# Queries and keys of each head as two float32r parts, with two heads in the halves of the partitions and GpSimd fetching them

## The reference

```
xn = layernorm(x, gamma, beta)
q, k, v = heads of xn @ Wq.T / 4, xn @ Wk.T, xn @ Wv.T      # 16 heads of 16
scores = q @ k.T + rel[h, clip(i - j, 0, 128)], masked to i >= j
y = softmax(scores) @ v ;  out = x + y @ Wo.T
```

## Time and profile before

| | us |
|---|---|
| median of 3 runs | 2771.97 |
| the profiled execution | 2777.85 |
| its span | 2776.0 |
| TensorE busy | 2217.6 |
| VectorE busy | 1620.4 |
| ScalarE busy | 969.2 |
| GpSimd busy | 453.9 |
| granted TensorE clock, mean | 0.863 |

### The profile page before, as it was taken

How to read it: one execution, slowest core, us unless ns; L and a number is a source line. 1 busy time by engine, 2 the same in 40 slices (tenths; PEclk the granted TensorE clock), 3 DMA queues, 4 the chain that set the end, 5 groups by cost and what they waited for, 6 DMA issues and landing times.

```text
span 2776.0 us, 39998 instructions
## 1 busy us (share of the span) xinstructions
PE 2217.6 (80%) x13342; PEld 1613.4 (58%) x13342; DVE 1620.4 (58%) x4577; ACT 969.2 (35%) x1964; POOL 453.9 (16%) x402
## 2 busy tenths in 40 slices
PE   4489999908999857999994276378999999999476
PEld 2478888806888736888883144324444454444254
DVE  6744443353555675433444897266866766875695
ACT  4122233203333331232331331325555556556321
POOL 4320000040000134000003553411011011000242
PEclk8799999958999878999997555669999999999755
DMA  7110101020000122001002100242322323230001
GB/s 237 41 59 26 28 28 32 22 76 1 1 1 1 35 83 73 28 28 32 28 28 60 49 12 0 61 65 59 48 42 53 48 47 63 37 43 2 5 22 39
DMA packets 83735, 114.14 MB, mean 41 GB/s; under 512 B 12162, under 2 KB 74020, under 8 KB 80420
## 3 DMA queue, kind: packets, MB, share of 16 engines
q1 hardware_dynamic: 77396, 94.53, 15.5%
q0 software_dynamic: 6144, 17.05, 1.9%
HBM read 68.90 MB, written 42.64 MB: 40 GB/s over the span
## 4 chain that ended last, share of the span: by engine, by line
PE 63%; DVE 21%; ACT 5%; issue 5%; DMA 3%; POOL 2%; another core or an unknown queue 1%; SPq 0%; ACTq 0%; DVEq 0%; POOLq 0%
PE psum L774 9%; PE psum L776 9%; PE psum L775 9%; PE psum L122 5%; PE psum L2097 4%; PE psum L123 4%; PE psum L124 4%; PE psum L2076 4%; PE psum L2056 3%; PE psum L861 3%; PE psum L2080 3%; DVE junk L1961 2%; PE psum L1426 2%; DVE m L1949 1%; DVE stats L155 1%
## 5 line engine op out<-in xcount | busy, mean ns | idle before, releaser
L1898 ACT ACTIVATE pt<-psum 128x512 f32<-128x512 f32 (+3 forms) x768 | 338.9, 491 | 283.2 <-DVE psum L1987 196.2
L739 DVE SCALAR_TENSOR_TENSOR h<-psum,xg,sg 128x128 f32<-128x128 f32 x592 | 166.9, 345 | 415.2 <-PE psum L861 415.2
L774 PE MATMUL psum<-w_hi,xt_hi 128*128 (+1 forms) x720 | 286.3, 398 | 33.7 <-DVE xt_lo L704 33.7
L548 ACT ACTIVATE sg<-psum 128x512 f32<-128x512 f32 x180 | 107.6, 598 | 584.0 <-PE psum L776 543.0
L775 PE MATMUL psum<-w_lo,xt_hi 128*128 (+1 forms) x720 | 284.5, 395 | 0.0
L776 PE MATMUL psum<-w_hi,xt_lo 128*128 (+1 forms) x720 | 284.5, 395 | 0.0
L2056 PE MATMUL psum<-ks,qs 96*128 96x512 bf16 (+3 forms) x768 | 232.9, 342 | 49.7 <-DMA ks<-qk_scr 19.9
L2076 PE MATMUL psum<-qs,ks 99*128 99x512 bf16 (+3 forms) x768 | 236.8, 332 | 18.4 <-ACT pt L1898 11.4
L774 PE MATMUL psum<-w_hi,ht_hi 128*128 (+1 forms) x720 | 220.5, 306 | 8.3 <-DVE x L754 8.0
L1961 DVE CUSTOM_DVE_ANT_0 junk<-psum,band_q 128x256 bf16<-128x256 f32 (+1 forms) x512 | 204.8, 400 | 22.3 <-PE psum L2056 12.0
L776 PE MATMUL psum<-w_hi,ht_lo 128*128 (+1 forms) x720 | 205.9, 286 | 0.0
(11 more groups left out here) (281 smaller groups left out, 4884.4 us busy)
## 6 DMA issues: line engine op xcount, KB each, us to landing
xg<-w_dram SPq DMA_DIRECT2D x54, 256.0 KB, 3.3
qk_scr<-parts SPq DMA_DIRECT2D x32, 384.0 KB, 2.5
qs<-qk_scr SPq DMA_DIRECT2D x96, 128.0 KB, 7.0
ks<-qk_scr SPq DMA_DIRECT2D x96, 128.0 KB, 7.7
xg<-rows_in SPq DMA_DIRECT2D x74, 132.0 KB, 2.2
rows_out<-yb SPq DMA_DIRECT2D x74, 128.0 KB, 1.7
x<-x_dram SPq DMA_DIRECT2D x4, 1024.0 KB, 9.3
out_dram<-x SPq DMA_DIRECT2D x4, 1024.0 KB, 4.4
```

The source lines that it names most:

```text
L739: ins = dve.scalar_tensor_tensor(out=h[i % 2][:, e, :], in0=u[:, e, :], scalar=xg[j % XSLOT][:, at:at + 1], in1=sg[i % 2][:, e, :], op0=AL ...
L774: pe.matmul(out, a[0], b[0], start=first, stop=False)
L1898: act.activation(pt[n % NPT][:, 0:q1 - q0], st_bank(n)[:, 0:q1 - q0], ACT.Exp).then_inc(*exped.up())
```

## The change

Queries and keys are kept as two float32r parts instead of three bf16 ones. ScalarE writes the first part and VectorE the second, so the second copy of ScalarE and the subtraction of GpSimd are gone. A head's stack has 3 x 16 = 48 rows (and 2 rows of the maximum in two float32r parts: 50 instead of 99). Heads 0 and 1 of a unit stand in partitions 0 to 63, heads 2 and 3 in 64 to 127. The maxima stream issues the products of head hh and head 2+hh one after the other, and the scores come in pairs (heads 3, 1 and heads 2, 0), with the bias products behind the pair as a token of their own (`band`). The steps of maxima now stand ahead of a pair, not behind a score; the stream leads by 1.4 units and is filled up to that lead at once. A projection token follows each second pair.

The fetches move from SyncE to GpSimd, and so does the transfer of the maxima into `qs`, now two transfers. The store of the parts stays on SyncE (512 KB instead of 384 KB each). The constant rows of `ks` are written by two copies of 32 rows x 2048 for each slot; they and the first three fetches stand ahead of the first `max_zero` in GpSimd's order. The custom instruction of VectorE writes into the PSUM bank that it reads, and its wait for the one before is gone. The diff, with up to 12 blanks of indentation taken off and cut to its core:

```diff
-HEAD_OF = (HG - 1, *range(HG - 1))
+HALF_ROWS = P // 2
+PAIR = HG // 2
+HEAD_OF = (HG - 1, 1, 2, 0)
+QK_PARTS = [(0, 0), (0, 1), (1, 0)]
+ROWS = DH * len(QK_PARTS)
+NPART = 2
...
+    yield [("max_zero", u)]
+    for hh in range(PAIR):
         for i in QORDER:
-            step = [("max_far", (u, h, i))] if spans(i)[3] else []
-            yield first + step + [("max", (u, h, i))]
-            first = []
+            if spans(i)[3]:
+                yield [("max_far", (u, half * PAIR + hh, i)) for half in range(2)]
+            yield [("max", (u, half * PAIR + hh, i)) for half in range(2)]
     yield [("max_row", u)]
...
-    yield [("max_rest", (u, 1))]
-    yield [("max_part", (u, 2))]
     yield [("max_out", u)]
...
-            yield [("score", (u, cell, pos))]
+        for pos in range(0, HG, 2):
+            yield [("score", (u, cell, pos)), ("score", (u, cell, pos + 1)), ("band", (u, cell, pos))]
...
-order = sum(project(0), []) + [("load", u) for u in range(min(NR, NHG))]
+order = [("ones", 0)] + sum(project(0), []) + [("load", 0)]
+for u in range(1, NR):
+    order += [("ones", u), ("load", u)]
...
-more()
-order.append(("ones", 0))
-steps, lead = HG * NCELL, 1.5
-per_u = HG * BT + 7
+steps, lead = PAIR * NCELL, 1.4
...
     for tokens in attend(u):
-        order.extend(tokens)
         if tokens[0][0] == "value":
+            order.extend(tokens)
             placed.add(tokens[0])
             continue
-        if taken[0] < (u + lead + step / steps) * per_u:
+        while taken[0] < min((u + lead + step / steps) * per_u, len(stream)):
             more()
+        order.extend(tokens)
         order.extend(next(tail, []))
-        if step % 3 == 0:
+        if step % 2 == 0:
             order.extend(next(proj, []))
...
-    qk_scr = nc.dram_tensor("qk_scr", (2, 2, 3, D, SEQ), BF16, kind="Internal").ap()
-    m_scr = nc.dram_tensor("m_scr", (2, 3, HG * BT, P), BF16, kind="Internal").ap()
+    qk_scr = nc.dram_tensor("qk_scr", (2, 2, NPART, D, SEQ), F32R, kind="Internal").ap()
+    m_scr = nc.dram_tensor("m_scr", (2, NPART, HG * BT, P), F32R, kind="Internal").ap()
...
-    qs = [sb(st, f"qs{i}", [KS_ROWS + MROWS, HG, SEQ], BF16) for i in range(NR)]
-    ks = [sb(st, f"ks{i}", [KS_ROWS + MROWS, HG, SEQ], BF16) for i in range(NR)]
+    qs, ks = ([sb(st, f"{n}{i}", [P, PAIR, SEQ], F32R) for i in range(NR)] for n in ("qs", "ks"))
+    unit = sb(st, "unit", [P, 1])
...
-    pt = [sb(st, f"pt{i}", [P, BANK]) for i in range(NPT)]
+    widest = [max(min((c + 1) * BANK, SEQ) - max(j * P, c * BANK) for j, c in CELLS[i::3]) for i in range(3)]
+    pt = [sb(st, f"pt{i}", [P, widest[i // HG]]) for i in range(NPT)]
...
-    parts = sb(st, "parts", [P, 3, KD, CH], BF16)
+    parts = sb(st, "parts", [P, NPART, KD, CH], F32R)
...
-    junk = sb(st, "junk", [P, 2 * P], BF16)
...
-    mparts = sb(st, "mparts", [HG * BT, 3, P], BF16)
+    mparts = sb(st, "mparts", [HG * BT, NPART, P], F32R)
...
+    def half_of(h):
+
+        return h // PAIR * HALF_ROWS, h % PAIR
...
-                sp.wait_ge(*part2(i + 1))
+                sp.wait_ge(*qk_lo(i + 1))
                 sp.dma_start(qk_scr[b % 2, n, :, o * P:(o + 1) * P, c * CH:(c + 1) * CH].rearrange(
-                    "i p s -> p i s"), parts[:, :, o, :]).then_inc(*S.dma(f"scr_out{n}{o}").up())
-            elif kind == "load":
-                b, g = divmod(i, NHG)
-                par, slot = b % 2, i % NR
-                for n in range(2):
-                    for o in range(KD):
-                        sp.wait_ge(*S.dma(f"scr_out{n}{o}")(CB * (b + 1)))
-                if i >= NR:
-                    sp.wait_ge(*score((i - NR + 1) * NCELL * HG))
-                for s0, pair in enumerate(SLOTS):
-                    for n, dst in enumerate((qs[slot], ks[slot])):
-                        src = qk_scr[par, n, pair[n], g * HG * DH:(g + 1) * HG * DH, :]
-                        sp.dma_start(dst[s0 * DH:(s0 + 1) * DH, :, :].rearrange("p h s -> p (h s)"),
-                                     src.rearrange("(d h) s -> d (h s)", h=HG)
-                                     ).then_inc(*S.dma(f"stack_in{slot}").up())
+                    "i p s -> p i s").bitcast(F32), parts[:, :, o, :].bitcast(F32)).then_inc(*S.dma(f"scr_out{n}{o}").up())
...
+                sp.wait_ge(*max_part(NPART * (i + 1)))
+                sp.dma_start(m_scr[i % 2].rearrange("i c p -> c i p").bitcast(F32),
+                             mparts[:, :, :].bitcast(F32)).then_inc(*S.dma("m_out").up())
...
-            elif kind == "qk":
-                bc, n, o, _ = qk_of(i)
-                pool.wait_ge(*part1(i + 1))
-                pool.tensor_tensor(parts[:, 2, o, :], rests[o][:, :], parts[:, 1, o, :],
-                                   ALU.subtract).then_inc(*part2.up())
+            elif kind == "load":
+                b, g = divmod(i, NHG)
+                slot = i % NR
+                pool.wait_ge(*ones_ok(2 * slot + 2))
+                for n in range(2):
+                    for o in range(KD):
+                        pool.wait_ge(*S.dma(f"scr_out{n}{o}")(CB * (b + 1)))
+                if i >= NR:
+                    pool.wait_ge(*score((i - NR + 1) * NCELL * HG))
+                for s0, pair in enumerate(QK_PARTS):
+                    for n, dst in enumerate((qs[slot], ks[slot])):
+                        for half in range(2):
+                            r0 = half * HALF_ROWS + s0 * DH
+                            src = qk_scr[b % 2, n, pair[n], (2 * g + half) * PAIR * DH:
+                                         (2 * g + half + 1) * PAIR * DH, :]
+                            pool.dma_start(dst[r0:r0 + DH, :, :].rearrange("p h s -> p (h s)"),
+                                           src.rearrange("(d h) s -> d (h s)", h=PAIR)
+                                           ).then_inc(*S.dma(f"stack_in{slot}").up())
+            elif kind == "max_out":
+                pool.wait_ge(*S.dma("m_out")(i + 1))
+                for half in range(2):
+                    r0 = half * HALF_ROWS + ROWS
+                    src = m_scr[i % 2][:, half * PAIR * BT:(half + 1) * PAIR * BT, :]
+                    pool.dma_start(qs[i % NR][r0:r0 + NPART, :, :].rearrange("i h s -> i (h s)"),
+                                   src.rearrange("i c p -> i (c p)")
+                                   ).then_inc(*S.dma(f"m_in{i % 2}").up())
...
             elif kind == "ones":
-                pool.wait_ge(*max_zero(1))
-                for r, k in enumerate(ks):
-                    pool.memset(k[KS_ROWS:KS_ROWS + MROWS, :, :], 1.0).then_inc(*ones_ok.up())
-                    pool.wait_ge(*ones_ok(r + 1))
+                if i == 0:
+                    pool.memset(unit[:, :], 1.0).then_inc(*S("unit").up())
+                    pool.wait_ge(*S("unit")(1))
+                else:
+                    pool.wait_ge(*xt_lo(KD * CB))
+                for half in range(2):
+                    rows = slice(half * HALF_ROWS + MQ, half * HALF_ROWS + 2 * MQ)
+                    pool.tensor_copy(ks[i][rows, :, :], unit[rows, :].unsqueeze(2).to_broadcast(
+                        [MQ, PAIR, SEQ])).then_inc(*ones_ok.up())
+                    pool.wait_ge(*ones_ok(2 * i + half + 1))
...
                 act.wait_ge(*proj(bc * PROJ + i % (2 * KD) + 1))
                 act.activation(parts[:, 0, o, :], mx_ring.bank((kind, i)), ACT.Copy,
-                               scale=scale).then_inc(*part0.up())
-                act.wait_ge(*rest_ok(i + 1))
-                act.activation(parts[:, 1, o, :], rests[o][:, :], ACT.Copy).then_inc(*part1.up())
+                               scale=scale).then_inc(*qk_hi.up())
...
-                if n == 0:
-                    dve.wait_ge(*xt_lo(KD * bc + o + 1))
-                else:
-                    dve.wait_ge(*part2(i - KD + 1))
-                dve.wait_ge(*part0(i + 1))
-                dve.scalar_tensor_tensor(out=rests[o][:, :], in0=mx_ring.bank((kind, i)), scalar=scale,
-                                         in1=parts[:, 0, o, :], op0=ALU.mult,
-                                         op1=ALU.subtract).then_inc(*rest_ok.up())
+                dve.wait_ge(*qk_hi(i + 1))
+                dve.scalar_tensor_tensor(out=parts[:, 1, o, :], in0=mx_ring.bank((kind, i)), scalar=scale,
+                                         in1=parts[:, 0, o, :].bitcast(F32), op0=ALU.mult,
+                                         op1=ALU.subtract).then_inc(*qk_lo.up())
...
-                if n:
-                    dve.wait_ge(*near_max(n))
+                banded = bank[:, far - cut:w - cut]
                 dve.tensor_tensor_reduce(
-                    junk[:, 0:bw], bank[:, far - cut:w - cut],
-                    band_q[:, u % NHG * HG + h, 2 * P - bw:2 * P], 1.0, LOWEST, ALU.add, ALU.max,
-                    m3[u % 2][:, h * BT + t, 2:3]).then_inc(*near_max.up())
+                    banded, banded, band_q[:, u % NHG * HG + h, 2 * P - bw:2 * P], 1.0, LOWEST, ALU.add,
```

(32 more changed lines are left out.)

33 lines of the change are left out of this document (10 added, 23 removed).

## The result

The changed kernel takes 3027.71 us, the median of four runs (3024.54 to 3032.68), against 2773.28 for the kernel before: ratio 1.0918, interval 1.0898 to 1.0937. It is 254 us slower. The sign and two of the mechanisms were as predicted; the size, 46 us, was not, and 3028 lies outside the range of 2685 to 2905.

A forecast was written before the change was run, and what follows sets the result against it. TensorE's list was taken to pace the steady part, VectorE not far under it. Start +19, long-unit fetches +22, short units +35, long units -30 gave +46 on 2777.85: 2824, or 2818 against the median; range 2685 to 2905 us.

The forecast's parts named there:

- Part 1, side by side: Scores and maxima on TensorE: a pair's products in different row halves overlap, 5.8 us less per unit.
- Rival B: Slower: the array's halves do not run side by side, 93 us more, 2911 us; chance 0.11.
- the change of shape: On TensorE, products of 64 rows alternating with 128: some 30 changes at 0.06 us, 1.8 us more per unit.
- Part 2, the distance between scores: Scores sharing a bank wait for exponentials: short units +3.5 us net, ten units +35; long ones -5, six units -30.
- the late bias of head 3: In near cells, VectorE's step of maxima ahead of the pair delays this bias by up to 0.8 us.
- the projections fill the gaps of long units: A projection token behind every first pair of a cell fills most gaps, leaving long units at -5 us each.
- Part 3, fetches on GpSimd: Fetches issued by GpSimd at 0.75 us each, mostly hidden, cost +19 us at the start and +22 in long units.
- the start: Before the first maxima and scores: 36 transfers and four copies ahead of `max_zero` cost +19 us, bounds +5 to +55.
- the long units: Units with projections: `add` behind a fetch delays `scale` and all exponentials, +22 us in total, bounds +9 and +65.
- Rival C: Slower: GpSimd's fetches at their high bounds, +36 and +43 us more, 2897 us; chance 0.10.
- Rival A: Faster: the array's time is what counts, short units fall to 33 us, 2690 us in all; chance 0.28.
- The signs I named: For being right: TensorE's waits for ScalarE over 80 us, short units of 40 us or more, TensorE busy under 90%.

The follow-up runs named there:

- all_rows: The changed kernel with every score and maximum product over all 128 rows (zero rows added), so no halves: 2917.38 us, ratio 1.0513.
- sync_fetch: The changed kernel with all fetches and the transfers of the maxima back on SyncE, as plain 4-byte copies: 3007.44 us, ratio 1.0842.
- pairs_bf16: The kernel before with only the changed kernel's order; bf16 stacks over the whole array and SyncE's fetches stay: 2916.83 us, ratio 1.0517.

## Why the prediction went wrong

**What bounds the kernel.** Right: TensorE's list paces the steady part, and ScalarE's exponentials are the ring behind it. Of the 254 us, some 120 are the clock, for which the sum had no term, and 143 are the order, for which it had a term of the right kind, several times too small. The rest of the sum nearly cancels.

**Part 1, side by side (-5.8 per unit).** The mechanism is right: pairs of 256 columns take the time of one. Among the 2850 distances at full clock, score behind score and maximum behind maximum are together 41.8 us shorter than in all_rows; all kinds that gain, 42.4 us. These distances are about nine units' worth, so 4.7 a unit come back of the 5.8. Rival B falls. What failed is the next sentence, the change of shape: I counted 30 per unit at 0.06 us, bracket 0 to 0.12, read off a value token. No row shows that such a token streams for four passes of 0.215, so its excess of 0.12 is no reading of the change; behind a value product the halves add 0.00. In a short unit of the changed kernel there are 42 changes, and the kinds of distances that lose, lose 40.7 us, 4.5 a unit instead of 1.8. That alone eats the gain of running side by side. (The Trainium skill, TensorEngine Tiling (Array Packing), Tiling Modes, says that changing the mode drains the engine. The 8.6 us for 85 changes agree with a drain; I had priced its result at 29 us, 2847.)

**The clock: not in my sum at all. This is the step that failed.** A short unit went from 48.9 to 50.2 us at clock 1.00 (all_rows) to 55.2 to 60.7 at 0.72 to 0.81. The 110 us between the two kernels are the clock: at full clock the same work takes the same time in both, and the distances at half clock account for 118 us. I had read the 1.00 of the earlier trace rows as given. It belongs to that mix of products.

**Part 2, the distance between scores (+3.5 per short unit, -5 per long one).** The chain of 1.54 us against a shorter distance was the right mechanism. The size failed at two places, and this is the second step that failed. I put the late bias of head 3 at up to 0.8 us and took the sum "below the middle", since VectorE had a fifth of its time free; the runs give 81 of 143 us to exactly that step. Order alone makes a short unit 10.6 to 12.1 us longer. And I let the projections fill the gaps of long units: with order alone two of them take 130.1 us against 118.8, 5.7 more each. 10 x 11.4 + 6 x 5.7 = 148, against 143 measured, where the sum had +35 and -30 with Part 1 in it. A stall in front of a score is not filled by a token that stands behind it in the same list.

**Part 3, fetches on GpSimd (+41).** The price of one was too high, the start came out nearly right, and the long units were over-priced. GpSimd's groups in the changed kernel:

```profile
L1835 POOL DMA_DIRECT2D qs<-qk_scr x96 | 47.6, 503 | 293.4 <-PE psum L2094 276.1 <-DMA qk_scr<-parts 14.0 <-issue 2.3
L1835 POOL DMA_DIRECT2D ks<-qk_scr x96 | 46.9, 498 | 0.0
```

0.50 us each, not 0.75: nearly SyncE's price. The start:

```profile
1785.44 1.15 POOL L1835 DMA_DIRECT2D qs<-qk_scr  x2 [14.04 <-DMA qk_scr<-parts]
...
1791.39 3.84 POOL L1858 CAST ks<-unit 32x2048 fp32r<-32x2048 f32 x2
...
1800.35 1.19 PE L2064 MATMUL psum<-ks,qs 48*128 48x512 f32 x3 [18.33 <-DMA ks<-qk_scr]
...
1811.80 1.29 DVE L1958 TENSOR_REDUCE m<-psum 128x1 f32<-128x512 f32 x2 [29.74 <-POOL m L1849]
...
1854.30 0.90 PE L2083 MATMUL psum<-qs,ks 50*128 50x512 f32 x2
```

The first three products of maxima are there at 1800.35, but VectorE's first maximum waits for `max_zero` (L1849), behind the 36 fetches, as predicted. The stages ahead end at different times in different runs, so start times in two runs can't be compared directly. From the last product of the linear layer (L1426, at 1733.72 before, 1725.56 in the changed kernel, 1726.10 in sync_fetch) the first maximum comes after 78.3, 86.2 and 74.0 us, and the first score after 110.2, 128.7 and 113.5. The first score is thus 18.5 us later than before, and I had +19 for the start. That is partly luck: a fetch costs 0.50 and a copy 1.9 us (I had 2.5), but the fetches begin only 2.5 us earlier where I had allowed 6, and the order by itself delays the first score by 9 us (pairs_bf16), where I had 3. GpSimd's share is 128.7 - 113.5 = 15.2 us, three quarters of the 20 that all its fetches cost. Some 5 are left for the long units, not 22. Rival C falls.

**Rival A** fell on the side that I gave for it: the waits of scores for ScalarE are 19.6 us in 31, 0.6 us on average and up to 1.5, over the 0.3 us that I had set. **The signs I named**: TensorE's busy share under 90% (88 to 90%) and short units over 40 us came true. TensorE's waits for ScalarE "over 80 us" did not: in 2060 to 2560 us they are 38.7 us for weight loads of scores, the row to be held against the 78.5 of the earlier trace rows, and 19.6 for the products, against 6.2 before. In all_rows, with the same list at full clock, they are 50.0 and 30.7. So part of the waits shrank because TensorE itself had slowed down, and then a smaller wait is no sign that the stall is gone.

**Open.** Why the clock falls. The runs show that it falls most when maxima and scores are both in halves in float32r, somewhat when they are in different halves in bf16 (156 us at half speed), and little or not at all with the order alone, with one kind in halves or with the whole array. In the runs where it falls, products overlap. Whether it is the overlap itself that brings it down was not isolated.

## What to carry to other kernels

Count how often a list changes between products over part of the rows and over all of them, and charge each change on the busiest engine (here 0.07 us on average in bf16, 0.10 to 0.11 in float32r, nothing behind a value product); in this kernel packing two small products gave back what the changes cost, and no more. In a ring of few buffers, what stands ahead of a producer on the engine that finishes its data decides: here filler behind the critical token cost 81 us less than filler in front of it. When two traces have the same list, lay them side by side product by product and sort the distances by clock: that tells a slower clock from slower work. And look at the granted clock of a trial before believing a sum of durations: a clock of 1.00 in the old profile belongs to the old mix.

## What the runs showed of the hardware

The granted clock alternates between its two levels, 1.00 and 0.50 (2.4 and 1.2 GHz), under a TensorE that is busy 97 to 98% of the time in either case: units of the same instructions took 44.1 us or 68.4. Two products in different halves of the rows start together even if they belong to different banks and lines. GpSimd issues a direct transfer of 16 rows in 0.50 us, half of the 0.97 of its indirect one. SyncE can move float32r tiles as plain float32 words (sync_fetch), and the kernel's output stays right.
